# Second half of a vision tower: next slot's rows normalised one slot ahead, attention polynomials in front of the low halves, values behind the scores, three gelu high halves cast by VectorE

## The chip, the core and the metric

The kernel runs on one core of a Trainium2 chip. The metric is the device time of one execution in microseconds. Before the change it is 833.44 us, the median of 3 runs (833.27 to 834.65). Engines are named as in the profile: PE (TensorE, matrix products; PEld its weight loads), DVE (VectorE), ACT (ScalarE), POOL (GpSimd), SP (the queue of transfers).

## The reference

64 images of 128 x 128 become 64 tokens each of 256 features. Four residual steps follow: softmax attention with a learned choice of keys, a routed feed-forward with 8 experts, causal "polymax" attention, and a gelu feed-forward with ternary weights.

```python
h = tok(x)                                  # patches of 16x16 times W, + b
h = h + sparse_softmax_attn(layernorm(h))   # 16 heads, 25 of 64 keys kept
h = h + routed_ffn(layernorm(h))            # 2 of 8 experts, plus shared silu ffn
# polymax attention
q, k, v = split(layernorm(h) @ W_attn)
att = q @ k.T / 4, causal
att = (x > 0 ? x**2 + 1 : x in [-100, 0] ? -0.01 * x + 1 : 0) / 1000
h = h + (att @ v) @ W_proj
# gelu feed-forward, w_t = sign(w) * (|w| > 0.5 * mean|w|)
z = layernorm(h)
g = gelu((z / (rms(z) + 1e-8)) @ w_up_t.T)
h = h + (g / (rms(g) + 1e-8)) @ w_down_t.T
```

## The kernel before

The 4096 tokens lie in SBUF as `H`, 32 tiles of 128 rows. Four tiles (8 images) are a slot; there are 8 slots. Phase A takes each slot through embedding, softmax attention and the shared part of the routed step. Phase B, from about 437 us, takes each slot `g` through the polymax attention (B1 projections, B2 scores, polynomials, values, output projection) and the gelu feed-forward (B3). The whole `H` is complete before phase B, apart from 8 rows of slot 7 that slot 5 adds to. The experts' gates are worked off in slots 1 to 5.

There is no scheduler. Each engine has its program written out in order, in a function `slot_B` of its own, and semaphores join the five programs. `slot_B(0)` and `slot_B(1)` are written out, slots 2 to 4 are a loop, and slots 5, 6, 7 are written out again. `routed` is "first" in slot 1, "batch" in 2 to 4, "last" in 5. The stages overlap: in slot `g` PE still multiplies slot `g - 1`'s gelus by the down weights, and it makes slot `g + 1`'s projections and first scores.

PE's order in slot `g`: `B2_scores` of tiles 2, 3 (L690, L443); the down product of slot `g - 1`, tiles 0, 1, by the high halves of the gelus (`down_part`, L751); `gram` (L740), whose diagonal gives the mean squares of the gelus; the down product by the low halves (L751); `B2_values` of tiles 0, 1 (L707); transposes of the normalised rows of slot `g + 1` (L368); `B2_proj` (L717); the down product of tiles 2, 3 (L763); the gates' turn (L624); keys and queries of slot `g + 1` (L378); the experts' sums (L613); values 2, 3; first value projection (L327); `B2_proj` (L717); gates (L633); other value projections; transposes for B3 (L368); scores 0, 1 of slot `g + 1`; the up product (L730), one of 8 parts per gelu.

Every number is split in two 16-bit halves for PE. Of the gelus, `g32[f]` (f = 0 to 7) holds the result of ACT's gelu (L1055), `G_hi` the high half, cast by ACT (`g_high`, L1046), `G_lo` the low half, a subtraction on DVE (`g_parts`, L1728). The down product by high halves waits for `gh_out` at each `f`, `gram` for `gl_out`.

The rows of slot `g + 1` are normalised at the start of slot `g`: `stats3` on DVE (L1252, L1257, L1260), the power -1/2 on POOL (`p_rstd`, L1130), minus mean times that on DVE (`minus_mean3`, L1641), then four ACT instructions that write `xn1` (`a_norm3`, L993). PE's transposes wait for them. ACT then copies the turned values (`a_turned`, L998) and the transposes' high halves (`a_B1_x`, L1006); DVE subtracts for the low halves (`v_x3T`, L1652).

A tile's scores pass through ACT (`relus` L1032, `quads` L1042, `lins` L1037) and DVE (`poly`, L1665 and L1671). For tiles 0, 1 DVE does the squares (`v_quads`, L1677) and one linear part (`v_lin`, L1683). `norm4` on DVE (L1264) normalises the rows for B3, `a_B3_x` (L1093) and `v_x4T` (L1721) are the halves of their transposes; PE starts these transposes once ACT has emptied bank 7 of slot `g + 1`'s first values (`a_B1_v`, L1022).

## Time and profile before

| | us |
|---|---|
| median of 3 runs | 833.44 |
| the profiled execution | 830.7 |
| its span, first to last instruction | 828.7 |
| PE busy in the span | 703.1 (85%) |
| DVE busy | 617.9 (75%) |
| ACT busy | 428.4 (52%) |
| mean granted clock of TensorE | 0.926 of 2.4 GHz |

A slot of phase B is about 48 us. Times in the rows count from the start of the span. A timeline row gives the start, the length (of all that are merged in it), engine, line and operands, how many, and in brackets how long the engine stood idle ahead of it and who ended that. Instructions overlap a little in issue, so a duration is best read as the distance to the next start. A granted clock of 1.00 is 2.4 GHz, of 0.50 it is 1.2 GHz. PE shows fp32 products of one tile as two rows' worth each (x8 for four).

### The profile page before, as it was taken

The numbers are of one execution on the slowest core, as the hardware profiler recorded it, in microseconds if no ns is written. First come the engines' busy times: TensorE is split into PE (matmuls) and PEld (weight loads), VectorE is DVE, ScalarE is ACT, GpSimd is POOL, SyncE is SP. The second block draws the span as 40 slices with busy tenths as digits, with TensorE's granted clock in tenths as the row PEclk, the third lists the DMA queues.
The fourth block names the chain that finished last, engine by engine and source line by source line (L and its number), as shares of the span: only waits on it lengthen the run. The fifth ranks groups of instructions, "written<-read, shape, count | busy, mean of one in ns | idle before, by whom it ended". The sixth has DMA issues, their size and how long they took to land.

```text
span 828.7 us, 26974 instructions
## 1 busy us (share of the span) xinstructions
PE 703.1 (85%) x11581; PEld 495.5 (60%) x11581; DVE 617.9 (75%) x1393; ACT 428.4 (52%) x653; POOL 85.5 (10%) x76
## 2 busy tenths in 40 slices
PE   5878999999999999947756889899898989888766
PEld 4565766667676767634454556575566656465534
DVE  6676979787888888786595578968877786677543
ACT  4535454555555554544214575938566493656413
POOL 0100212121212020100000000000000000000000
PEclk9889999999999999977865999999998999999959
DMA  9034202020202002000000000000000000000000
GB/s 320 20 127 131 78 0 76 0 76 0 76 0 76 0 0 103 3 1 1 1 1 2 2 3 28 3 27 2 25 0 0 25 2 27 2 28 2 27 3 27
DMA packets 8546, 27.40 MB, mean 33 GB/s; under 512 B 3616, under 2 KB 4384, under 8 KB 6944
## 3 DMA queue, kind: packets, MB, share of 16 engines
q1 hardware_dynamic: 8480, 26.42, 8.8%
q8 instruction: 53, 0.87, 0.4%
q14 instruction: 13, 0.11, 0.0%
HBM read 22.22 MB, written 4.19 MB: 32 GB/s over the span
## 4 chain that ended last, share of the span: by engine, by line
PE 42%; issue 22%; DVE 21%; ACT 9%; POOL 2%; SPq 2%; DMA 1%; DVEq 0%; POOLq 0%; ACTq 0%
PE PS L378 7%; PE PS L327 6%; PE PS L389 5%; PE PS L488 4%; PE PS L717 3%; PE PS L368 3%; PE PS L477 3%; PE PS L432 3%; DVE mx L1343 3%; DVE Pm L1349 3%; PE PS L763 2%; PE PS L443 2%; SPq L307 2%; DMA work<-in_x 1%; PE PS L345 1%
## 5 line engine op out<-in xcount | busy, mean ns | idle before, releaser
L368 PE MATMUL PS<-ident_s,xn 128*128 128x128 f32 x256 | 50.3, 311 | 33.5 <-DVE xn L1264 16.5
L919 ACT ACTIVATE PT<-PS 128x512 f32<-128x512 f32 x64 | 36.7, 596 | 70.1 <-PE PS L477 70.1
L730 PE MATMUL PS<-xT,wqkv_h 128*128 128x512 f16 x256 | 63.1, 391 | 5.7 <-ACT w_s L1055 4.2
L368 PEld LDWEIGHTS PS<-ident_s,xn 128*128 128x128 f32 x256 | 32.0, 150 | 46.8 <-DVE xn L1264 15.5
L327 PE MATMUL PS<-tokW_h,w_s 128*128 128x256 f16 x504 | 58.5, 273 | 0.0
L912 ACT ACTIVATE Pm<-Pm 128x1024 f32<-128x1024 f32 x32 | 33.1, 1054 | 46.8 <-DVE Pm L1349 46.8
L327 PEld LDWEIGHTS PS<-tokW_h,w_s 128*128 128x128 f16 x504 | 48.7, 98 | 5.8
L443 PE MATMUL PS<-kM,qT 32*64 32x128 f32 x2048 | 50.2, 285 | 0.0
L378 PE MATMUL PS<-xT,wat_h 128*128 128x512 f16 x192 | 46.2, 400 | 4.5 <-DVE xT L1652 4.5
L730 PEld LDWEIGHTS PS<-xT,wqkv_h 128*128 128x128 f16 x256 | 22.6, 100 | 44.1 <-ACT w_s L1055 17.7
L1252 DVE BATCH_NORM_STATS2 st<-H 128x6 f32 (+1 forms) x128 | 46.3, 414 | 2.5
L477 PE MATMUL PS<-ident_s,Pm 128*128 128x128 f32 x256 | 41.1, 297 | 7.3 <-DVE Pm L1349 7.0
L1689 DVE TENSOR_TENSOR H<-H,PS 128x512 f32<-128x512 f32 (+1 forms) x16 | 11.0, 687 | 48.0 <-PE PS L717 48.0
L1130 POOL TENSOR_TENSOR rstd<-ve,mhalf 128x4 f32<-128x4 f32 x16 | 16.1, 1008 | 275.7 <-DVE ve L1260 275.7
L488 PE MATMUL PS<-vbuf,PT 128*64 128x34 f32 x1024 | 41.6, 233 | 3.4 <-ACT PT L919 3.4
L488 PEld LDWEIGHTS PS<-vbuf,PT 128*64 128x64 f32 x1024 | 36.1, 145 | 13.3 <-ACT PT L919 7.5
L1343 DVE TENSOR_REDUCE mx<-PS 128x16 f32<-128x1024 f32 x32 | 39.0, 1218 | 5.3 <-PE PS L443 5.3
L443 PEld LDWEIGHTS PS<-kM,qT 32*64 32x64 f32 x2048 | 42.8, 136 | 0.0
L717 PE MATMUL PS<-wpr_s,xT 128*128 128x256 f32 x128 | 41.4, 481 | 1.4 <-ACT xT L998 1.4
L1349 DVE TENSOR_TENSOR Pm<-PS,mx 128x1024 f32<-128x1024 f32 x32 | 39.2, 1225 | 3.5
L1728 DVE TENSOR_TENSOR work<-w_s,work 128x512 f16<-128x512 f32 x48 | 32.2, 688 | 11.2 <-ACT work L1046 11.2
L378 PEld LDWEIGHTS PS<-xT,wat_h 128*128 128x128 f16 x192 | 19.1, 102 | 28.8 <-issue 9.5
(250 smaller groups left out, 1610.9 us busy)
## 6 DMA issues: line engine op xcount, KB each, us to landing
work<-in_x SPq DMA_DIRECT2D x7, 1536.0 KB, 6.3
out<-H SPq DMA_DIRECT2D x8, 512.0 KB, 2.6
w_s<-in_w SPq DMA_DIRECT2D x3, 1024.0 KB, 6.9
work<-in_x SPq DMA_DIRECT2D x3, 512.0 KB, 5.7
wup_s<-in_wup SPq DMA_DIRECT2D x1, 1024.0 KB, 6.4
wdn_s<-in_wdn SPq DMA_DIRECT2D x1, 1024.0 KB, 8.4
w_s<-in_tokW SPq DMA_DIRECT2D x3, 256.0 KB, 4.1
wup_s<-in_wqkv SPq DMA_DIRECT2D x1, 768.0 KB, 7.7
```

The source lines that it names most:

```text
L327: m = pe.matmul(dst, halves_[xi][:, k, rows], w[:, wi, k, cols], start=(n == 0), stop=(n == 3 * chunks - 1))
L368: m = pe.transpose(PS[:, bank, t * P:(t + 1) * P], xn[:, t, c * P:(c + 1) * P], ident_s[:, :])
L378: m = pe.matmul(PS[0:cols, bank, :], w[:, wi, c, col:col + cols], x[xi][:, c, 0:TOK], start=(n == 0), stop=(n == 3 * C - 1))
L389: m = pe.matmul(PS[:, bank, :], w[:, wi, c, col:col + P], x[xi][:, c, 0:TOK], start=(c == 0 and wi + xi == 0), stop=(c == C - 1 and xi == 1))
L443: m = pe.matmul(PS[b * L:(b + 1) * L, i, hb + c * P:hb + (c + 1) * P], left[r, c, at:at + L], right[r, c, :, at:at + L], start=False, stop ...
L477: m = pe.transpose(PS[:, TURN_BANKS[t][half], hp * P:(hp + 1) * P], Pm[:, t % 2, at:at + P], ident_s[:, :])
L488: m = pe.matmul(PS[b * L:(b + 1) * L, 6 + t % 2, hp * 2 * VW:(hp + 1) * 2 * VW], PT[:, t % 2, hp, b * L:(b + 1) * L], Vb[:, 2 * t + b, hp, ...
L717: m = pe.matmul(PS[:, bank, (t % 2) * E:(t % 2 + 1) * E], yT[:, t, c, :], wpr_s[:, c, :], start=(c == 0), stop=(c == C - 1))
L730: m = pe.matmul(PS[:, UP_BANKS[f % 3], :], wup_h[:, c, f * P:(f + 1) * P], part[:, c, :], start=(k == 0), stop=(k == 2 * C - 1))
L1252: dve.bn_stats(st_[:, t, :], H[:, TILES * g + t, :]).then_inc(in_st, 1)
L1343: dve.tensor_reduce(mx[:, t % 2, :].rearrange("p (i h) -> p i h", i=4), PS[:, 0:4, hb:hb + 256].rearrange("p i (h k) -> p i h k", k=L), AX ...
L1349: dve.tensor_tensor(Pm[:, t % 2, :].rearrange("p (i h k) -> p i h k", i=4, k=L), PS[:, 0:4, hb:hb + 256].rearrange("p i (h k) -> p i h k", ...
```

## The change

1. `stats3`, `p_rstd`, `minus_mean3` and `a_norm3` for slot `g + 2` are done in slot `g` (slots 0 to 5) and not for slot `g + 1` at its start. On DVE the statistics stand behind `norm4(g, 0)`, the last step behind `stats4(g, 1)`; on ACT the four instructions stand between `a_turned(g, 1)` and `a_B1_v(g + 1, 0)`. In slot 5 all of it comes after the rows that the routed step adds, and ACT's part behind `a_B1_v(6, 0)`.
2. In DVE's order `poly(g + 1, 0)` and `poly(g + 1, 1)` stand in front of all of `g_parts`.
3. In PE's order `B2_values(g, 0)` stands in front of the down product by high halves.
4. `G_hi` of f = 5, 6, 7 is cast by DVE inside `g_parts`, each with a wait of its own, and no longer by ACT.
5. `v_x3T` and `silus` stand together in front of `weighted_hots` and `projected`.

```diff
+        ACT_HIGH = 5
...
                 for f in range(NF):
                     if high and t == 0:
-                        pe.wait_ge(gh_out, NF * g + f + 1)
+                        if f < ACT_HIGH:
+                            pe.wait_ge(gh_out, ACT_HIGH * g + f + 1)
+                        else:
+                            pe.wait_ge(ghv_out, (NF - ACT_HIGH) * g + f - ACT_HIGH + 1)
...
                 if prev:
                     pe.wait_ge(g_ok, NF * g)
+                    B2_values(g, 0)
                     for t in (0, 1):
                         down_part(g - 1, t, G_hi, True)
...
                     pe.wait_ge(racc_ok, 1)
-                B2_values(g, 0)
+                    B2_values(g, 0)
...
             def g_high(g, f):
-                act.wait_ge(g_ok, NF * g + f + 1)
-                act.activation(G_hi[:, f, :], g32[f], ACT.Copy).then_inc(gh_out, 1)
+                if f < ACT_HIGH:
+                    act.wait_ge(g_ok, NF * g + f + 1)
+                    act.activation(G_hi[:, f, :], g32[f], ACT.Copy).then_inc(gh_out, 1)
...
-                if nxt:
+                if not prev:
                     a_norm3(g + 1)
                 a_turned(g, 0)
...
                 a_turned(g, 1)
+                if ahead and routed != "last":
+                    a_norm3(g + 2)
                 if nxt:
                     a_B1_v(g + 1, 0)
                 if routed in ("first", "batch"):
                     routed_tanh(g, 0)
+                if routed == "last":
+                    a_norm3(g + 2)
                 a_B3_x(g)
...
                 for f in range(f0, f1):
-                    dve.wait_ge(gh_out, NF * g + f + 1)
+                    if f < ACT_HIGH:
+                        dve.wait_ge(gh_out, ACT_HIGH * g + f + 1)
+                    else:
+                        dve.wait_ge(g_ok, NF * g + f + 1)
+                        dve.tensor_copy(G_hi[:, f, :], g32[f]).then_inc(ghv_out, 1)
+                        dve.wait_ge(ghv_out, (NF - ACT_HIGH) * g + f - ACT_HIGH + 1)
                     dve.tensor_tensor(G_lo[:, f, :], g32[f], G_hi[:, f, :], ALU.subtract)\
...
-                if nxt:
-                    stats3(g + 1)
                 if prev:
                     mean_squares(g - 1)
-                if nxt:
+                else:
+                    stats3(g + 1)
                     minus_mean3(g + 1)
                 if routed in ("batch", "last"):
                     silus(g - 1)
+                if nxt:
+                    v_x3T(g + 1)
+                if routed in ("batch", "last"):
                     weighted_hots(g)
                 projected(g, 0, 5)
...
                 norm4(g, 0)
+                if ahead and routed != "last":
+                    stats3(g + 2)
                 projected(g, 1, 4)
                 stats4(g, 1)
+                if ahead and routed != "last":
+                    minus_mean3(g + 2)
...
+                if routed == "last":
+                    stats3(g + 2)
+                    minus_mean3(g + 2)
                 v_x4T(g)
                 if nxt:
                     v_quads(g + 1, 0)
                     v_quads(g + 1, 1)
                     v_lin(g + 1)
-                g_parts(g, 0, 4)
                 if nxt:
                     poly(g + 1, 0)
-                g_parts(g, 4, NF)
-                if nxt:
                     poly(g + 1, 1)
+                g_parts(g, 0, NF)
```

The left-out parts pass `ahead=False` to slots 6 and 7 on each engine and move POOL's `p_rstd` to stand between its two `p_ln4` (behind both in slot 5).

How the order reads, taken from slot 1, first before and then after in each pair. DVE at the end of slot 1, from the linear part of slot 2's first tiles; `th` and `hs` are the two tiles' polynomials, `work` the halves of the gelus:

```order
L1683 TENSOR_SCALAR late<-PS 128x1024
L1728 TENSOR_TENSOR work<-w_s,work 128x512 x4
L1665 SCALAR_TENSOR_TENSOR th<-u,th 128x1024
L1671 SCALAR_TENSOR_TENSOR Pm<-u,th 128x1024
L1728 TENSOR_TENSOR work<-w_s,work 128x512 x2
L1728 TENSOR_TENSOR work<-wqkv_h,work 128x512
L1728 TENSOR_TENSOR work<-tokW_h,work 128x512
L1665 SCALAR_TENSOR_TENSOR hs<-late,hs 128x1024
L1671 SCALAR_TENSOR_TENSOR Pm<-late,hs 128x1024
L1252 BN_STATS st<-H 128x6 x4
```

```order
L1696 TENSOR_SCALAR late<-PS 128x1024
L1678 SCALAR_TENSOR_TENSOR th<-u,th 128x1024
L1684 SCALAR_TENSOR_TENSOR Pm<-u,th 128x1024
L1678 SCALAR_TENSOR_TENSOR hs<-late,hs 128x1024
L1684 SCALAR_TENSOR_TENSOR Pm<-late,hs 128x1024
L1746 TENSOR_TENSOR work<-w_s,work 128x512 x5
L1744 CAST work<-w_s 128x512
L1746 TENSOR_TENSOR work<-w_s,work 128x512
L1744 CAST work<-wqkv_h 128x512
L1746 TENSOR_TENSOR work<-wqkv_h,work 128x512
L1744 CAST work<-tokW_h 128x512
L1746 TENSOR_TENSOR work<-tokW_h,work 128x512
```

Both polynomials now come first, then five subtractions, then cast and subtraction in turn three times; the four BN_STATS of the next slot's rows are no longer behind them.

ACT in slot 1, from the keys' and queries' copies to the gates' tanh (`wdn_s`); `vbuf` is the first value copy, `xn` the rows to be normalised:

```order
L1017 ACTIVATE kM<-PS,par_s 128x512 x4
L998 ACTIVATE xT<-PS 128x2x4x64
L1022 ACTIVATE vbuf<-PS 128x16x2x16
L988 ACTIVATE wdn_s<-wup_s 128x1024
L1093 ACTIVATE xT<-PS 128x512 x2
```

```order
L1022 ACTIVATE kM<-PS,par_s 128x512 x4
L1003 ACTIVATE xT<-PS 128x2x4x64
L998 ACTIVATE xn<-H,nm,rstd 128x256 x4
L1027 ACTIVATE vbuf<-PS 128x16x2x16
L993 ACTIVATE wdn_s<-wup_s 128x1024
L1103 ACTIVATE xT<-PS 128x512 x2
```

The four `xn` instructions now stand in front of `vbuf`, for which PE's next transposes wait.

PE at the start of slot 1, from the last scores:

```order
L443 MATMUL PS<-kM,qT 64x128 x16
L751 MATMUL PS<-tokW_h,work 128x256 x16
L740 MATMUL PS<-work 32x64 x128
L751 MATMUL PS<-tokW_h,work 128x256 x16
L707 MATMUL PS<-Pm,vbuf 32x64 x64
L368 MATMUL PS<-ident_s,xn 128x128 x8
```

```order
L444 MATMUL PS<-kM,qT 64x128 x16
L708 MATMUL PS<-Pm,vbuf 32x64 x64
L755 MATMUL PS<-tokW_h,work 128x256 x16
L741 MATMUL PS<-work 32x64 x128
L755 MATMUL PS<-tokW_h,work 128x256 x16
L369 MATMUL PS<-ident_s,xn 128x128 x8
```

The values (`Pm,vbuf`) moved from behind the down products to the front of them.

## Rows read from the trace of the kernel before

**Rows 1.** The page, section 1: busy time of each engine over the span.

```profile
PE 703.1 (85%) x11581; PEld 495.5 (60%) x11581; DVE 617.9 (75%) x1393; ACT 428.4 (52%) x653; POOL 85.5 (10%) x76
```

**Rows 2.** Timeline of PE, junction of slots 3 and 4, then slot 6 (start, length, idle before).

```profile
624.33 2.10 PE L751 MATMUL PS<-tokW_h,work 128*128 128x256 f16 x16 [0.37 <-ACT tokW_h L1055]
626.36 1.30 PE L740 MATMUL PS<-work 128*32 128x64 f16 x128
...
629.44 1.61 PE L707 MATMUL PS<-Pm,vbuf 64*32 64x64 f32 x128
633.58 0.33 PE L368 MATMUL PS<-ident_s,xn 128*128 128x128 f32 x1 [2.54 <-ACT xn L993]
...
734.96 0.76 PE L368 MATMUL PS<-ident_s,xn 128*128 128x128 f32 x5 [0.16 <-ACT xn L993]
735.56 1.89 PE L717 MATMUL PS<-wpr_s,xT 128*128 128x256 f32 x8
```

**Rows 3.** Timeline of DVE, same junction.

```profile
619.07 1.33 DVE L1728 TENSOR_TENSOR work<-w_s,work 128x512 f16<-128x512 f32 x2
...
622.33 1.22 DVE L1665 SCALAR_TENSOR_TENSOR th<-u,th 128x1024 f32<-128x1024 f32 x1
...
624.81 1.28 DVE L1728 TENSOR_TENSOR work<-w_s,work 128x512 f16<-128x512 f32 x2
...
629.61 1.40 DVE L1252 BATCH_NORM_STATS2 st<-H 128x6 f32 x4
```

**Rows 4.** Timeline of ACT, same junction.

```profile
624.00 0.70 ACT L1046 ACTIVATE work<-wqkv_h 128x512 f16<-128x512 f32 x1
...
631.75 1.01 ACT L1037 ACTIVATE late<-PS 128x1024 f32<-128x1024 f32 x1
632.93 2.08 ACT L993 ACTIVATE xn<-H,nm,rstd 128x256 f32 x4 [0.17 <-DVE nm L1641]
```

**Rows 5.** Groups of DVE instructions by form: busy, mean ns.

```profile
L1245 DVE TENSOR_SCALAR work<-wup_s,nthr 128x2048 f32<-128x2048 f32 x1 | 1.3, 1290 | 0.0
...
L1449 DVE CAST selb<-PS 128x512 bf16<-128x512 f32 x1 | 0.7, 681 | 0.0
...
L1234 DVE CAST cmaskb<-cmask_s 128x384 bf16<-128x384 f32 x1 | 0.4, 355 | 0.0
```

**Rows 6.** Timelines of PE, DVE and ACT before slot 3's gelus; DVE in slot 1.

```profile
611.01 1.09 PE L368 MATMUL PS<-ident_s,xn 128*128 128x128 f32 x6 [0.46 <-DVE xn L1264]
...
606.52 0.69 DVE L1689 TENSOR_TENSOR H<-H,PS 128x512 f32 x1 [2.13 <-PE PS L717]
...
608.46 0.16 DVE L1700 COPY vr<-mv 128x2 f32<-128x2 f32 x1
...
609.06 0.60 ACT L1022 ACTIVATE vbuf<-PS 128x512 f32<-128x512 f32 x1 [4.73 <-PE PS L327]
...
614.33 1.02 ACT L1032 ACTIVATE th<-PS 128x1024 f32<-128x1024 f32 x1
...
509.30 0.69 DVE L1689 TENSOR_TENSOR H<-H,PS 128x512 f32<-128x512 f32 x1 [0.38 <-PE PS L717]
```

**Rows 7.** Timelines of DVE and ACT before slot 5's gelus.

```profile
709.64 0.41 DVE L1634 TENSOR_TENSOR H<-H,PS 8x256 f32<-8x256 f32 x1 [1.19 <-PE PS L645]
...
710.40 0.60 ACT L1022 ACTIVATE vbuf<-PS 128x512 f32<-128x512 f32 x1 [8.78 <-PE PS L327]
...
714.34 1.02 ACT L1032 ACTIVATE th<-PS 128x1024 f32<-128x1024 f32 x1 [0.62 <-PE PS L443]
```

**Rows 8.** Windows: us, busy PE, PEld, DVE, ACT, POOL, granted clock, DMA, GB/s.

```profile
538.30:541.70 3.40, 3.40 (x11) 2.59 (x9) 0.89 (x1) 0.91 (x2) 0.00 (x0) 0.51 0.00 0
...
630.50:633.90 3.40, 0.86 (x55) 0.52 (x32) 2.86 (x18) 3.19 (x5) 1.98 (x2) 1.00 0.00 0
...
633.90:640.70 6.80, 6.60 (x22) 4.80 (x22) 3.17 (x5) 2.78 (x6) 0.00 (x0) 0.50 0.00 0
...
777.30:780.70 3.40, 3.40 (x11) 2.42 (x10) 0.22 (x1) 0.00 (x0) 0.00 (x0) 0.50 0.00 0
```

More of the change, by code:

```diff
@@ L778, in B3_down_last, with slot_B @@
                             m.then_inc(dn_mm, 1)
-            def slot_B(g, prev, nxt, routed=None):
+            def slot_B(g, prev, nxt, routed=None, ahead=True):
                 B2_scores(g, 2)
@@ L865, in _ @@
             slot_B(LAST - 2, True, True, routed="last")
-            slot_B(LAST - 1, True, True)
-            slot_B(LAST, True, False)
+            slot_B(LAST - 1, True, True, ahead=False)
+            slot_B(LAST, True, False, ahead=False)
             B3_down_last(LAST)
@@ L1061, in a_B3, with slot_B @@
                 g_high(g, NF - 1)
-            def slot_B(g, prev, nxt, routed=None):
+            def slot_B(g, prev, nxt, routed=None, ahead=True):
                 for t in (2, 3):
@@ L1121, in _ @@
             slot_B(LAST - 2, True, True, routed="last")
-            slot_B(LAST - 1, True, True)
-            slot_B(LAST, True, False)
+            slot_B(LAST - 1, True, True, ahead=False)
+            slot_B(LAST, True, False, ahead=False)
         @block.gpsimd
@@ L1177, in p_rg, with slot_B @@
                 pool.tensor_tensor(rg[:, :], msq[:, :], phalf[:, :], ALU.pow).then_inc(rg_ok, 1)
-            def slot_B(g, prev, nxt, routed=None):
-                if nxt:
-                    p_rstd(ve3_ok, g + 2, ve, rstd, rstd3_ok)
+            def slot_B(g, prev, nxt, routed=None, ahead=True):
                 if prev:
@@ L1191, in _ @@
             slot_B(LAST - 2, True, True, routed="last")
-            slot_B(LAST - 1, True, True)
-            slot_B(LAST, True, False)
+            slot_B(LAST - 1, True, True, ahead=False)
+            slot_B(LAST, True, False, ahead=False)
             p_rg(LAST)
@@ L1772, in slot_B @@
                     one_over_rms(g - 1)
-                if nxt:
-                    v_x3T(g + 1)
-                if prev:
                     ffn_out(g - 1)
@@ L1782, in slot_B @@
                 norm4(g, 0)
+                if ahead and routed != "last":
+                    stats3(g + 2)
                 projected(g, 1, 4)
                 stats4(g, 1)
+                if ahead and routed != "last":
+                    minus_mean3(g + 2)
                 if routed == "last":
@@ L1793, in slot_B @@
                     routed_rows_in()
+                if routed == "last":
+                    stats3(g + 2)
+                    minus_mean3(g + 2)
                 v_x4T(g)
@@ L1845, in _ @@
             slot_B(LAST - 2, True, True, routed="last")
-            slot_B(LAST - 1, True, True)
-            slot_B(LAST, True, False)
+            slot_B(LAST - 1, True, True, ahead=False)
+            slot_B(LAST, True, False, ahead=False)
             mean_squares(LAST)
```

8 lines of the change are left out of this document (5 added, 3 removed).

## The prediction

> **What bounds the kernel now.** I read the page first, then the timelines of PE, DVE and ACT over one slot of phase B, and last the windows with the granted clock. PE is busy for 703.1 of 828.7 us [rows 1], and within a slot it rests at few places, so a change pays only where it moves PE. I measure everything from the start of ACT's first relu of the next slot (614.33 [rows 6]), call that t, and follow slot 3 into slot 4. Behind the last scores, which end 0.37 before 624.33, so at 623.96, PE does 16 down products with high halves in 2.03, gram and low halves in 3.08 (626.36 to 629.44) and the values in 1.61, without a break, and ends at 631.05 [rows 2]. Then it stands for 2.54 until the rows of the next slot are normalised. That wait is a chain: DVE's statistics start at 629.61, behind the second polynomial [rows 3], POOL and one DVE step follow, and ACT starts its four normalisations at 632.93, 2.08 us for four [rows 4]. PE's transposes go at ACT's pace for the first few. In slot 6 the last five take 0.60 (734.96 to 735.56) [rows 2], that is 0.12 each; all eight at ACT's pace take about 2.0. So the output projection could start at 633.58 + 2.0 = 635.6, t + 21.2.
>
> The second thing to see is the clock. In the stretch in which PE idled (630.50 to 633.90) it was busy for 0.86, and right behind it the clock was at 0.50, 1.2 GHz, for 6.8 us [rows 8]. The projection there took 3.62 where it takes 1.89 in slot 6 [rows 2, 8]. I count five low stretches of 3.4 us in slots 2 to 5 and one in slot 7 at the same place (the first, the double one and the last are shown). A low stretch full of work costs 1.7, so the six cost about 10 us.
>
> **The change part by part: the junction of two slots.** The wait for the rows goes: they are ready a slot early. What is late next is the high halves. DVE starts its part behind the linear step at 619.07 [rows 3]. A polynomial lasts 2.48 (622.33 to 624.81), a subtraction 0.60 (half of 1.20 from 624.81 on, two with 0.09 of overlap). Two polynomials and five subtractions: 619.07 + 4.96 + 3.0 = 627.05. Only then comes the cast of f = 5.
>
> No row shows a cast of 128x512 between two SBUF tiles. From the sides: 128x512 out of PSUM took 0.68, 128x384 in SBUF 0.36, and 2048 elements of a one-input operation 1.29 [rows 5]. The line through the last two is 0.14 + 0.00056 per element, 0.42 for 512; I take that, since it rests on SBUF rows, and keep 0.36 and 0.69. (The Trainium skill, VectorE: DVE Perf Modes, section on the perf-mode tiers, has fp32 copies in SBUF at two elements per cycle and any PSUM operand of fp32 at one; by that the 0.68 row doesn't bear on this cast and the sum below stands; by the row alone it would be 5.7 higher. The trace agrees as far as the 1.29 goes.) A dependent pair starts 0.12 after the first ends (622.33 + 1.22 to 623.67). So the casts end at 627.05 + 0.42 = 627.5, then every 1.1 (0.42 + 0.12 + 0.60): 628.6 and 629.7.
>
> (The same page, in its section on the DRAIN, says that semaphores between chained operations cost nothing. The 0.12 in the row is against it. By the page f = 7 would land 0.2 to 0.3 earlier, some 2 us over seven junctions.)
>
> PE now does the values first, 623.96 to 625.56; both polynomials are done by 624.1, so they don't wait. Five high products until 626.2, then waits of 1.3, 1.0 and 1.0 for f = 5, 6, 7. With 9 products of 0.127 behind the last cast it is 630.9, with gram and low halves (the last low half is there at 630.5) 634.0, with eight unhindered transposes of 0.12 635.0. ACT isn't late: its last casts (624.00 to 625.2 [rows 4]) fall away, its last linear step ends 2 us before 632.8. So t + 20.7 instead of t + 21.2: 0.5 gained, not 4.5. For six junctions (slots 1 to 6) -3.3 with 0.55 each. Into slot 7 there is no row to be normalised; there PE waited only for ACT's linear step (632.8 in the same frame) and the turned values, 0.6 more, t + 19.1, against 634.0, t + 19.7, now: +0.6.
>
> **In front of the gelus.** ACT's four instructions now stand in front of `a_B1_v`, and wait for `minus_mean3`, which DVE issues behind the statistics of B3's second half. These end at 608.6 [rows 6], because `projected` waited 2.13 for PE. So ACT normalises from 608.8 to 610.9, and the value copy, before at 609.06, ends at 611.45. Behind the waiting instruction stand on ACT that copy, the tanh, the high halves of the transposes, then the relus and gelus. PE waits for the copy before it transposes: it resumed fully at 611.01 after 0.46, now it starts all eight at 611.5. ACT: tanh 1.0, high halves as the transposes end (613.6), value copy 0.5, tanh 1.0, relu at 615.1 instead of 614.33: +0.75. The gelus are ACT's pace, so nothing gives it back. The new statistics on DVE, 1.84 (like 629.61 to 631.45), fit into the 2.13 idle. Slots 0, 2, 3, 4: +3.0, slot 0 being an estimate by the others. In slot 1 `projected` had only 0.38 of idle in front of it [rows 6]; the first normalisation of B3 ends at 508.9 there. With `v_x3T` (1.2) taken out of the chain ahead it ends at 507.7, the statistics at 509.55, while the product is there at 508.7 (0.55 earlier than before): 0.85 of them is on the path, and slot 1 costs 0.75 + 0.85 = 1.6.
>
> In slot 5 the chain is serial: rows added at 709.64 to 710.05, statistics to 712.0, POOL 1.1, `nm` at 713.3, ACT 713.45 to 715.5, high halves 1.0, value copy 0.5, relu at 717.1 instead of 714.34 [rows 7]: +2.8.
>
> POOL's power for two slots ahead takes 1.0 between two of its own that stand 6 us apart: nothing. Nothing moves on SP. The end of slot 7 is PE's work; casts on an idle DVE hide beside it: nothing. `v_x3T` earlier frees DVE, but PE comes no earlier: nothing outside slot 1.
>
> **Sum without the clock:** -3.3 + 0.6 + 3.0 + 1.6 + 2.8 = +4.7. **The clock:** the idle time at a junction is now three waits of about 1 us with one product between, 3.3 in all, instead of 2.5 in one piece and thin transposes behind. PE is as empty as before for as long, so I expect the low stretches to stay in kind, and some to begin inside the idle time, where they cost less. I take one of the six as saved, -1.7, and as bounds none left (-10) and two more (+3.4), the second because slot 5 has a new wait of 3 us. In all +3.0: span 828.7 to 831.7, the profiled execution 830.7 to 833.7. The runs' median is 2.7 above that one execution, so I forecast 833.44 + 3.0, 836.4.
>
> **The rivals.**
> - The clock decides. If the three short waits don't bring the clock down, all low stretches go, 833.4 + 4.7 - 10 = 828. From fewer than three left on (4.7 / 1.7) the kernel is faster. For it: in slot 6 1.50 of idle and paced transposes left the clock up (the projection at 735.56 took 1.89). Against: PE's work between the waits is one product of 0.13 each.
> - The cast is slow, 0.69 as out of PSUM: 0.27 more for each of three casts at seven junctions, +5.7, 842. For it is only the one row with 512 elements; the SBUF rows speak against it.
> - The casts of f = 5 to 7 are on the path but the normalisation isn't: if ACT's early part were hidden (as it would be if `minus_mean3` came before 607), 3.0 + 1.6 fall away: about 832. Against it is the written order, which puts it behind `stats4`.
> - Gains and losses meet: three or four low stretches fewer, 833 to 834, no change.
>
> **How the numbers follow.** Forecast as described 0.47; slow cast 0.11; no change 0.20; clock up or norm hidden 0.22. A change under 0.2% (831.8 to 835.1) is one that a measurement can't tell from none. The forecast's own range is 834 to 840. The range for 8 in 10 takes in the next cases on both sides: 831 to 841.5. Faster 0.23, same 0.20, slower 0.57.
>
> **What would show it.** In the new profile: PE idle in front of the down products (L755), three times near 1 us per junction, released by DVE's casts; the casts at about 420 ns; no idle in front of the transposes of the next rows; ACT's `xn` instructions starting 0.1 behind `nm`, and PE idle 1.3 in front of B3's transposes in slots 0 to 4; some 3 us in slot 5 before the up product. The forecast is wrong if the casts end before PE wants them, if PE doesn't wait for the value copy, or if the clock stays at 1.00 across the junctions.

## The result, and the profile after

| | before | after |
|---|---|---|
| median of 18 runs, us | 832.89 (828.65 to 836.62) | 827.96 (824.38 to 834.26) |
| the profiled execution | 830.7 | 828.74 |
| its span | 828.7 | 826.6 |
| mean granted clock | 0.926 | 0.924 |

The ratio is 0.9946, with a 95% interval of 0.9924 to 0.9968: the change is 0.54% faster, 4.9 us between the medians. I had forecast 3 slower, and the range began at 831. The forecast was wrong in sign. The two profiled executions differ by 2.0 only, and their spans by 2.1, of which 1.8 arise before slot 1's first relu (470.90 and 469.09 us), nearly all in code that is the same; so single spans don't carry the comparison here, and I compare slots. Executions in the slower of the chip's two states are left out of the ratios here and below, so a ratio may differ a little from that of the medians.

The answer to [rows 1], busy time of each engine in the profile of after:

```profile
PE 697.0 (84%) x11581; PEld 493.8 (60%) x11581; DVE 626.1 (76%) x1417; ACT 413.7 (50%) x629; POOL 89.3 (11%) x76
```

24 casts of 0.4 have moved from ACT to DVE. PE does the same instructions in 6 us less, which no edit asks for. 3.0 of these lie ahead of slot 1's first relu, 1.9 behind slot 7's projection, where the clock was 0.80 and not 0.73, and only 1.1 in the slots between.

The junction of slots 3 and 4, PE's timeline of after, to be laid beside [rows 2]. Here t, the start of the first relu, is 610.49:

```profile
620.07 1.60 PE L708 MATMUL PS<-Pm,vbuf 64*32 64x64 f32 x128
621.60 0.72 PE L755 MATMUL PS<-tokW_h,work 128*128 128x256 f16 x5
623.59 0.28 PE L755 MATMUL PS<-tokW_h,work 128*128 128x256 f16 x1 [1.26 <-DVE work L1744]
624.65 0.28 PE L755 MATMUL PS<-tokW_h,work 128*128 128x256 f16 x1 [0.78 <-DVE work L1744]
625.71 2.10 PE L755 MATMUL PS<-tokW_h,work 128*128 128x256 f16 x9 [0.78 <-DVE work L1744]
627.74 1.68 PE L741 MATMUL PS<-work 128*32 128x64 f16 x128
629.36 1.92 PE L755 MATMUL PS<-tokW_h,work 128*128 128x256 f16 x16
631.12 1.04 PE L369 MATMUL PS<-ident_s,xn 128*128 128x128 f32 x8
631.99 1.89 PE L718 MATMUL PS<-wpr_s,xT 128*128 128x256 f32 x8
```

DVE's timeline there, which answers to [rows 3]:

```profile
620.10 3.09 DVE L1746 TENSOR_TENSOR work<-w_s,work 128x512 f16<-128x512 f32 x5
623.11 0.42 DVE L1744 CAST work<-w_s 128x512 f16<-128x512 f32 x1
623.56 0.69 DVE L1746 TENSOR_TENSOR work<-w_s,work 128x512 f16<-128x512 f32 x1
```

And the windows of after over PE's three waits and over what follows them, to be laid beside [rows 8]:

```profile
624.00:627.40 3.40, 1.97 (x10) 1.28 (x10) 2.31 (x5) 2.55 (x4) 0.00 (x0) 0.73 0.00 0
627.40:630.80 3.40, 3.40 (x144) 2.87 (x143) 1.19 (x9) 0.00 (x0) 0.44 (x1) 0.77 0.00 0
```

The wait for the rows is gone as forecast, and three waits for DVE's casts, at 0.42 each, stand in its place. (The Trainium skill, VectorE: DVE Perf Modes, section on the perf-mode tiers, gives an fp32 copy in SBUF the rate on which my 0.42 stood; the row agrees.) What is new is where the low clock falls. Here it begins 0.1 before the last wait ends (elsewhere between 0.1 after that and, in slot 7, 1.1 before it) and lies on nine products, 2.10 long, and on `gram`, 1.68; at full clock these take 1.16 and 1.34 (rows of the filled kernel below). In before it lay on the full projection, which at full clock takes 1.89:

```profile
636.18 3.62 PE L717 MATMUL PS<-wpr_s,xT 128*128 128x256 f32 x8
```

The step from the cast at 623.11 to its subtraction at 623.56 is 0.45, so a dependent pair behind a cast loses only 0.03 and not the 0.12 that I had read off a pair of polynomial steps.

In front of the gelus, ACT and PE in slot 3 of after, which answer to [rows 6]:

```profile
604.71 2.07 ACT L998 ACTIVATE xn<-H,nm,rstd 128x256 f32 x4 [4.50 <-DVE nm L1654]
606.69 0.58 ACT L1027 ACTIVATE vbuf<-PS 128x512 f32<-128x512 f32 x1
...
610.49 1.03 ACT L1037 ACTIVATE th<-PS 128x1024 f32<-128x1024 f32 x1
...
607.32 1.09 PE L369 MATMUL PS<-ident_s,xn 128*128 128x128 f32 x8 [1.10 <-ACT vbuf L1027]
```

I had PE idle for 1.3 here in slots 0 to 4. It is 1.1 in slots 2 to 4, but 1.7 in slot 1 and 4.7 in slot 0.

### The profile page after: what moved, and what is told of

Its sections match the earlier page's. It is cut to its first block, busy times and chain, and to the rows that moved or that the text cites. A ratio compares the mean times of both kernels' runs of the same rounds, so it can differ in the third digit from the quotient of the medians.

```text
span 826.6 us, 27023 instructions
## 1 busy us (share of the span) xinstructions
PE 697.0 (84%) x11581; PEld 493.8 (60%) x11581; DVE 626.1 (76%) x1417; ACT 413.7 (50%) x629; POOL 89.3 (11%) x76
## 4 chain that ended last, share of the span: by engine, by line
PE 47%; DVE 28%; issue 10%; ACT 9%; SPq 3%; DMA 1%; POOL 1%; DVEq 0%; ACTq 0%; POOLq 0%
PE PS L379 7%; PE PS L328 6%; PE PS L390 5%; DVE work L1746 4%; PE PS L489 4%; PE PS L755 3%; PE PS L718 3%; PE PS L369 3%; PE PS L767 3%; PE PS L478 3%; DVE mx L1356 3%; DVE Pm L1362 3%; PE PS L433 2%; DVE hs L1678 2%; DVE th L1678 2%
## 5 line engine op out<-in xcount | busy, mean ns | idle before, releaser
L731 PE MATMUL PS<-xT,wqkv_h 128*128 128x512 f16 x256 | 65.2, 403 | 8.9 <-DVE xT L1734 4.6
L369 PE MATMUL PS<-ident_s,xn 128*128 128x128 f32 x256 | 42.6, 298 | 25.2 <-DVE xn L1277 12.6
L755 PE MATMUL PS<-tokW_h,work 128*128 128x256 f16 x224 | 37.1, 315 | 18.1 <-DVE work L1744 18.1
L444 PE MATMUL PS<-kM,qT 32*64 32x128 f32 x2048 | 52.0, 293 | 0.0
L379 PE MATMUL PS<-xT,wat_h 128*128 128x512 f16 x192 | 44.5, 390 | 2.5 <-DVE xT L1665 2.5
L755 PEld LDWEIGHTS PS<-tokW_h,work 128*128 128x128 f16 x224 | 22.9, 110 | 28.2 <-DVE work L1744 22.7
L478 PEld LDWEIGHTS PS<-ident_s,Pm 128*128 128x128 f32 x256 | 29.7, 149 | 10.4 <-issue 8.4
L718 PE MATMUL PS<-wpr_s,xT 128*128 128x256 f32 x128 | 33.9, 412 | 0.7 <-ACT xT L1003 0.7
```

Of the source, the lines that this page charges most:

```text
L369: m = pe.transpose(PS[:, bank, t * P:(t + 1) * P], xn[:, t, c * P:(c + 1) * P], ident_s[:, :])
L379: m = pe.matmul(PS[0:cols, bank, :], w[:, wi, c, col:col + cols], x[xi][:, c, 0:TOK], start=(n == 0), stop=(n == 3 * C - 1))
L444: m = pe.matmul(PS[b * L:(b + 1) * L, i, hb + c * P:hb + (c + 1) * P], left[r, c, at:at + L], right[r, c, :, at:at + L], start=False, stop ...
L478: m = pe.transpose(PS[:, TURN_BANKS[t][half], hp * P:(hp + 1) * P], Pm[:, t % 2, at:at + P], ident_s[:, :])
L718: m = pe.matmul(PS[:, bank, (t % 2) * E:(t % 2 + 1) * E], yT[:, t, c, :], wpr_s[:, c, :], start=(c == 0), stop=(c == C - 1))
L731: m = pe.matmul(PS[:, UP_BANKS[f % 3], :], wup_h[:, c, f * P:(f + 1) * P], part[:, c, :], start=(k == 0), stop=(k == 2 * C - 1))
```

## The slots, kernel by kernel

Below, T1 is the time from a slot's first relu t to the next output projection (the junction, 21.2 in my text), T2 the time from that projection to the next t. "Clean" is a slot in which no window shows a low clock. Both are starts read off the timelines, and a T1 is counted to the slot in which it ends. The T1 column covers slots 2 to 6. The mean granted clock is that of the stretch from 484 to 755 us (slots 1 to 6); "no releaser" is PE's idle time there that the waits put down to nothing.

| kernel | ratio to before | T1 clean | T2 clean, slots 2 to 4 | mean clock | no releaser, us |
|---|---|---|---|---|---|
| before | 1 | 21.2 | none (25.8 in the runs without part 1) | 0.97 | 2.3 |
| after | 0.9946 | 20.4 (slot 2 alone); 20.2 in kernels made from it | 26.03 | 0.96 | 0.5 |
| part 1 alone | 0.9904 | 19.4 to 19.6 | 26.05 | 0.97 | 2.0 |
| part 2 alone | 0.9830 | 20.4 | 25.76 | 0.99 | 1.0 |
| parts 2, 3 alone | 0.9906 | 20.4 (slot 5), 21.0 and 21.3 (slots 2, 6) | 25.75 | 0.97 | 5.9 |
| part 4 alone | 1.0057 | none (22.6 to 23.2) | 25.76 | 0.96 | 0 |
| part 1 undone | 0.9983 | 21.7 to 21.9 | 25.76 | 0.97 | 1.0 |
| part 3 undone | 1.0164 | none (23.1 to 23.9) | 26.04 | 0.94 | 0 |
| part 4 undone | 0.9779 | 17.8 (slots 3 to 5) | 26.05 | 0.99 | 5.6 |

Before and after are nearly alike in the mean clock, but not in what a low stretch costs at a junction nor in how many there are. In slots 3 to 5 of after, the T1 of 20.2 becomes 21.4 to 21.6 with a low stretch and T2 isn't touched; in before, T1 of 21.2 becomes 21.85 and T2 rises from 25.8 to 26.7, 27.4 and 28.0. Per slot that is 1.3 against 1.5 to 2.9. On the other hand after has seven low stretches between 484 and 755 us and before five (two of them back to back), and one of double length stands in front of slot 7's projection (T1 22.09 instead of 19.15). The whole way from slot 1's first relu to slot 7's projection, and the rest behind it, first before and then after:

```profile
470.90:776.94 306.04, 272.76 (x5266) 184.38 (x5264) 232.27 (x491) 195.33 (x297) 25.02 (x25) 0.97 0.03 12
776.94:828.70 51.76, 34.36 (x408) 22.23 (x408) 22.91 (x60) 10.16 (x19) 3.02 (x3) 0.73 0.06 22
```

```profile
469.09:776.57 307.48, 271.64 (x5267) 185.40 (x5266) 237.73 (x502) 180.25 (x272) 27.86 (x24) 0.95 0.03 12
776.57:826.60 50.03, 32.42 (x410) 20.84 (x408) 23.91 (x63) 8.69 (x16) 3.02 (x3) 0.80 0.06 22
```

So in this pair the slots take 1.4 longer after the change, at a mean clock of 0.95 instead of 0.97, although the clean times make them about 1.2 shorter (the sum in the section on the prediction, without slot 0). In these two executions the low clock costs after some 2.6 more there, not less.

## The experiments

Each is compared with the kernel before, run on the same chip. The intervals are of the ratio to it. The medians of the kernel before lie between 830.59 and 832.89 from chip to chip, so two experiments are compared by their ratios.

**Part 1 alone** (next rows normalised a slot ahead, in the kernel before).

```diff
-                if nxt:
-                    stats3(g + 1)
                 if prev:
                     mean_squares(g - 1)
...
                 norm4(g, 0)
+                if ahead and routed != "last":
+                    stats3(g + 2)
```

> The kernel before with part 1 alone: rows normalised a slot ahead; the polynomials, the values and all eight casts (on ACT) stand as before. My theory T: the wait of 2.5 us for the rows is what held a junction, and the casts on DVE gave most of that back. Then a junction here loses the wait (2.54) and the paced transposes (about 0.7): 6 x -3.2 = -19, against it about +4.5 in front of the gelus (0.3 in four slots, 2.6 in slot 5): 15 to 18 us faster than before, near 817, also well faster than after. Rival R (the casts on DVE are what helps ACT, the rows alone bring little): within 3 us of the changed kernel or slower. Rival C (the time follows the low stretches of the clock): the wait gone, they go too, and it is 20 us or more faster than before.

Measured 823.1 against 831.05, ratio 0.9904 (0.9866 to 0.9941): 8 faster, half of what T said, and far from C. That is 3.5 faster than after by the ratios, whose intervals overlap, so R's number isn't excluded; its reason, that the casts on DVE help, falls with the runs on part 4 below. T overlooked what comes next. PE, then ACT, in the junction of slots 3 and 4:

```profile
629.04 1.27 PE L368 MATMUL PS<-ident_s,xn 128*128 128x128 f32 x8 [1.81 <-ACT late L1037]
...
625.89 1.02 ACT L1032 ACTIVATE hs<-PS 128x1024 f32<-128x1024 f32 x1 [1.59 <-DVE Pm L1678]
```

With the rows there, PE waits 1.81 for ACT's last linear step; ACT waited 1.59 for DVE's second polynomial, which stood behind all low halves. Parts 1 and 2 belong together.

**Parts 2 and 3 alone, and part 2 alone.** Both take the polynomials to the front in DVE's order; the first also takes the values to the front in PE's.

```diff
-                g_parts(g, 0, 4)
                 if nxt:
                     poly(g + 1, 0)
-                g_parts(g, 4, NF)
-                if nxt:
                     poly(g + 1, 1)
+                g_parts(g, 0, NF)
```

> The kernel before with parts 2 and 3 alone: both polynomials in front of the low halves, values in front of the down product; all casts on ACT, rows normalised at the start of the slot. Theory T: DVE's statistics for the next rows start at the same time as before, since the sum of its work ahead is the same, so PE's wait for the rows stays and takes the same end: no change, within 2 us of before. Rival R (the new order itself is the gain): 4 to 6 us faster. Rival C: only the place of the idle time matters to the clock, some us either way with the cleanly clocked junction unchanged.

> The kernel before with part 2 alone: both polynomials in front of all low halves, everything else as before. With part 3 beside it 7.6 us were gained, which I had not expected. Reading of that trace: in the kernel before DVE stood still twice for 0.31 behind a gelu's cast and the second polynomial came only behind all low halves; without that its statistics for the next rows start 0.84 earlier (t + 14.44 instead of 15.28), and so do the rows. Theory T: this is the whole gain: 5 to 7 us faster than before, the place of the values is worth nothing while PE waits for the rows. Rival V (the values in front are the gain): within 2 us of before.

Measured 823.45, ratio 0.9906 (0.9871 to 0.9941), for the two parts; 816.29, ratio 0.9830 (0.9802 to 0.9857), for part 2 alone. The first refutes T as it stood (no change): the low halves of f = 2, 3 had waited twice 0.31 for ACT's casts. The second is the surprise of the study, and twice what its T said: the same DVE work, a clean T1 of 20.4 in both, and 6 us less by the ratios. PE in the same junction, part 2 alone:

```profile
620.35 0.30 PE L740 MATMUL PS<-work 128*32 128x64 f16 x16 [0.30 <-DVE work L1728]
620.95 0.30 PE L740 MATMUL PS<-work 128*32 128x64 f16 x16 [0.30 <-DVE work L1728]
621.55 0.30 PE L740 MATMUL PS<-work 128*32 128x64 f16 x16 [0.30 <-DVE work L1728]
...
623.64 1.61 PE L707 MATMUL PS<-Pm,vbuf 64*32 64x64 f32 x128
625.38 0.33 PE L368 MATMUL PS<-ident_s,xn 128*128 128x128 f32 x1
```

Its windows, and behind them PE's wait and the windows of the kernel with parts 2 and 3:

```profile
620.60:624.00 3.40, 2.80 (x92) 2.21 (x86) 3.29 (x19) 3.07 (x4) 0.62 (x1) 1.00 0.00 0
624.00:627.40 3.40, 2.77 (x118) 2.01 (x104) 2.82 (x4) 2.68 (x6) 1.36 (x2) 1.00 0.00 0
```

```profile
630.34 0.33 PE L368 MATMUL PS<-ident_s,xn 128*128 128x128 f32 x1 [1.68 <-ACT xn L994]
```

```profile
627.40:630.80 3.40, 1.59 (x13) 1.02 (x10) 2.86 (x18) 2.39 (x5) 1.98 (x2) 1.00 0.00 0
630.80:634.20 3.40, 3.04 (x10) 2.41 (x11) 2.29 (x2) 2.64 (x5) 0.00 (x0) 0.62 0.00 0
```

With gaps of 0.30 (three) and 0.17 (three) a junction the clock stays at 2.4 GHz through slots 1 to 4 of part 2 alone; with the values in front, the wait for the rows stands in one piece of 1.68, and in slots 3 and 4 the clock falls to 1.2 GHz right behind it (T1 21.0, T2 26.8). These two slots are 3.1 of the 5.1 by which the two traces differ between slot 1's first relu and slot 7's projection. The rest isn't all the clock: with the values in front PE is idle for 5.9 without a releaser and not for 1.0, and slot 2, with a clean clock, has a T1 of 21.0. Of the 14.6 that part 2 alone brings, 6 x 0.85 = 5 is T1; the other 9 are close to the 10 at which the prediction had put the low stretches of before. All of these are gone from the junctions; one in slot 5, at 693 us, stands elsewhere. That it is the long gap which brought the clock down is not shown: see the runs with one cast and with part 1 undone.

**Part 4 alone, and part 4 undone** (the three casts).

```diff
-        ACT_HIGH = 5
+        ACT_HIGH = NF
```

> The kernel before with part 4 alone: f = 5, 6, 7 cast by DVE, its order and PE's as before. Theory T: three casts of 0.42 stand in DVE's chain ahead of the statistics for the next rows, which PE waits for: 1.3 later in six junctions: 6 to 9 us slower than before. Behind parts 1 and 2 the same casts cost 15, because PE asks for the halves at once there. Rival R (ACT's relief pays by itself): faster than before. Rival P (a cast costs the same wherever it stands): 15 slower.

> The changed kernel with all eight high halves cast by ACT again (part 4 undone). Theory T: PE's three waits in front of f = 5, 6, 7 (1.26, 0.78, 0.78) go, and nothing takes their place before the transposes: junction shorter by 2.5 to 2.8 in slots 1 to 7, about 17 us faster than after, 810 to 813. Rival R (ACT needs the relief): ACT's casts then end too late for f = 5 to 7, and it is the same as after or slower. Rival C: the waits gone, the low stretches of the clock go as well, and it is 25 us faster than after.

Part 4 alone: 835.55, ratio 1.0057 (1.0037 to 1.0077), 4.7 slower, T1 1.35 longer as T says, with a low stretch in every junction from slot 2 on; the total is below its 6 to 9, and P (15) is refuted. The changed kernel without part 4: 812.87, ratio 0.9779 (0.9741 to 0.9816), inside T's 810 to 813. Its junction has no wait left:

```profile
621.55 1.38 PE L741 MATMUL PS<-work 128*32 128x64 f16 x128
622.86 1.92 PE L755 MATMUL PS<-tokW_h,work 128*128 128x256 f16 x16
624.92 1.10 PE L369 MATMUL PS<-ident_s,xn 128*128 128x128 f32 x8
```

So by the ratios the casts on DVE cost 14 here and 5 where the rows are late anyway. That ACT had to be relieved is refuted.

**One cast on DVE instead of three.** In the changed kernel:

```diff
-        ACT_HIGH = 5
+        ACT_HIGH = 7
```

> The changed kernel with one high half cast by DVE (f = 7) and seven by ACT. All eight on ACT gave 812.9 where three on DVE gave 828.0. Theory T (what costs is that a cast on DVE stands behind two polynomials and all subtractions in order, so that the last one is late): 624.03 + 7 x 0.6 + 0.42 = 628.65 in the frame of slot 3, where three casts end at 629.7 and PE asks at about 627; so one cast alone costs over half of what three do: 7 x 1.1 faster than after, 819 to 822. Rival (each cast costs its own 0.42 and gap, in proportion): a third of the cost, near 818 or less. Rival (ACT is relieved by one cast, DVE has the room): as fast as all on ACT, 813.

Measured 816.76, ratio 0.9810 (0.9784 to 0.9835). T1 is 19.3 in slots 3 and 4, where T's chain with 5.3 behind the cast makes 19.6, and the total 2 below T's range: four fifths of the 14 come back. The wait is in one piece, and the clock stays up around it (1.00 in all windows from 617.8 to 628.0, 0.99 in the mean), although it is no shorter than the 1.68 above:

```profile
621.78 1.16 PE L755 MATMUL PS<-tokW_h,work 128*128 128x256 f16 x9 [1.73 <-DVE work L1744]
```

T gave the order of the effect (more than in proportion, one cast costs 1.5 of T1 and three cost 2.4), not the total.

**Part 1 undone** (parts 2 to 4 stay).

```diff
-                if not prev:
+                if nxt:
                     a_norm3(g + 1)
```

> The changed kernel with the next rows normalised at the slot's start again (parts 2 to 4 stay). Theory T: with the casts in DVE's chain the rows are ready 1.3 later than with parts 2 and 3 alone, at t + 21.8 instead of 20.2 to 20.4 here: 6 x 1.4 = 8.4, less what part 1 costs in front of the gelus (3.6 in all): about 5 slower than after, near 833, the same as before the change. Rival A (part 1 costs what I forecast, 7.4 in all): 1 slower than after, 829. Rival C (low stretches as in the kernel before, on the projection): 8 to 10 slower.

Measured 829.14, ratio 0.9983 (0.9963 to 1.0003): 3 slower than after by the ratios, whose intervals just meet, where T said 5 and A 1; C is refuted. The junction is T's (21.84, forecast 21.8), and T2 is 25.76: part 1 costs 0.28 in slots 2 to 4, so rival A is wrong in its reason though nearest in its number. What makes T's 5 into 3 is likely the clock: slots 2 to 4 have no low stretch here, and in after slots 3, 4 and 5 have one each. Yet the waits for the casts are the same as in after, with paced transposes behind them. PE's waits and two windows in the junction of slots 3 and 4:

```profile
626.54 0.28 PE L755 MATMUL PS<-tokW_h,work 128*128 128x256 f16 x1 [1.27 <-DVE work L1737]
...
628.67 1.16 PE L755 MATMUL PS<-tokW_h,work 128*128 128x256 f16 x9 [0.78 <-DVE work L1737]
```

```profile
624.00:627.40 3.40, 1.56 (x69) 0.96 (x48) 3.37 (x7) 3.34 (x5) 0.00 (x0) 1.00 0.00 0
627.40:630.80 3.40, 2.42 (x122) 1.94 (x122) 3.33 (x12) 1.65 (x2) 0.00 (x0) 1.00 0.00 0
```

So the length and number of the waits don't settle by themselves whether the clock falls.

**Part 3 undone** (the values behind the low halves again, in the changed kernel).

```diff
                     pe.wait_ge(g_ok, NF * g)
-                    B2_values(g, 0)
...
                         down_part(g - 1, t, G_lo, False)
+                    B2_values(g, 0)
```

> The changed kernel with the values back behind the down product's low halves (part 3 undone). Theory T, from starts in the trace of after: the last cast is ready at t + 15.2 whatever PE does before; 9 products 1.1, gram 1.3, low halves 1.8, values 1.55, transposes 0.9 behind it make t + 21.8 instead of 20.2: 1.5 in seven junctions, about 10 us slower than after, near 838. Rival C (PE's waits move to another place and the clock stays up, as it did where part 2 stood alone): the 10 are given back by it, and it is the same as after or faster.

Measured 845.79, ratio 1.0164 (1.0137 to 1.0191), 18 slower than after by the ratios and 8 beyond T; C is refuted. PE and the windows:

```profile
633.23 0.28 PE L755 MATMUL PS<-tokW_h,work 128*128 128x256 f16 x1 [2.81 <-DVE work L1744]
...
635.36 2.10 PE L755 MATMUL PS<-tokW_h,work 128*128 128x256 f16 x9 [0.78 <-DVE work L1744]
```

```profile
630.00:633.40 3.40, 0.59 (x5) 0.25 (x3) 3.37 (x7) 3.37 (x4) 0.00 (x0) 1.00 0.00 0
633.40:636.80 3.40, 1.84 (x9) 1.13 (x9) 2.56 (x5) 2.32 (x3) 0.00 (x0) 0.69 0.00 0
```

The waits are 4.4 a slot and every junction up to slot 6 has its low stretch, two of them 6.8 long. Part 3 is worth 18 behind parts 1, 2 and 4, and costs 6 behind part 2 alone. It pays where it fills a wait.

**Part 5 undone** (`v_x3T` behind `one_over_rms` again).

> The changed kernel with the low halves of the next rows (v_x3T) back behind one_over_rms, as before the change (part 5 undone). My prediction put this part at nothing outside slot 1. From the trace of after: in slot 0 PE's keys and queries start 2.07 earlier, but the time is lost again at B3's transposes, whose rows come last; so at most 1 us there, and in slots 1 to 5 the wait of PE for the halves may come back at 0.3 to 0.5 each. Theory T: 1 to 3 us slower than after. Rival (the part is worth nothing): same within 0.5.

Measured 827.65, ratio 0.9943 (0.9922 to 0.9964), the same as after: the rival holds and T (1 to 3 slower) doesn't. In slot 0 the low halves bring PE forward, as I had not seen, but it waits for B3's rows in any case; in slot 1 T2 is 0.5 longer. The prediction's "nothing outside slot 1" holds for the total.

**Filling PE's waits.** To test the clock by itself, PE multiplies something that nobody reads, in front of its waits in the changed kernel.

```diff
+                            fill(9 if f == ACT_HIGH else 6)
                             pe.wait_ge(ghv_out, (NF - ACT_HIGH) * g + f - ACT_HIGH + 1)
```

> The changed kernel with 21 more products a slot (9, 6, 6), whose result nobody reads, put by PE into a free part of bank 6 in front of its waits for f = 5, 6, 7. At 0.127 each they fill the waits of 1.26, 0.78, 0.78 and should move nothing by themselves. Theory C (PE's idle time at the junction brings the low stretch behind it, which costs 1.1 in slots 3 to 5 and more in slot 7): the low stretches at the junctions go, 4 to 8 us faster than after. Rival (the low stretches come anyway, wherever PE is thin): same as after, or up to 2 slower by products that end late.

> The changed kernel with 10 products of 512 columns (4, 3, 3) in front of the waits for f = 5, 6, 7, in place of the 21 products of 256: about the same length of filled time, half the instructions. The 21 kept the clock up through slots 1 to 5, but PE stood for 10.8 us without a releaser in the profile, and in the loop's last turn its instructions were loaded again, which in no other run happened. Theory I (the instructions cost it, by their number: the loop no longer stays in PE's store): with 20 fewer no loads in the loop's second and third turn, the stalls back at 0.5 to 3, and the time 3 to 6 us faster than after, from the low stretches that go. Rival (filling costs by itself, or the loop is too long already): at or above after's time.

With 21 products of 256 columns: 837.88, ratio 1.0044 (1.0009 to 1.0079), 8 slower than after by the ratios where C said 4 to 8 faster, and yet the low stretches between 484 and 700 are all gone in the profiled execution. With 10 of 512: 825.6, ratio 0.9928 (0.9901 to 0.9955). That is 1.5 under after by the ratios, too little to tell, and short of Theory I's 3 to 6. But the junction of slots 3 and 4 in the second is the cleanest comparison of the study, since its waits and after's end at the same time (the product behind the last cast starts at 625.70 here and at 625.71 in after):

```profile
624.75 0.81 PE L749 MATMUL PS<-wqkv_h 128*128 128x512 f16 x3
625.70 1.16 PE L761 MATMUL PS<-tokW_h,work 128*128 128x256 f16 x9
626.78 1.34 PE L741 MATMUL PS<-work 128*32 128x64 f16 x128
628.06 1.92 PE L761 MATMUL PS<-tokW_h,work 128*128 128x256 f16 x16
...
630.69 1.68 PE L718 MATMUL PS<-wpr_s,xT 128*128 128x256 f32 x7
```

The projection starts at 630.69 and not at 631.99: 1.30 is what the clock takes from after at this junction. In the profile it was given back in slot 2 and late: 4.7 without a releaser, and low stretches in slots 5 and 6. What the 21 products cost is told below.

**The normalisation moved out of the way**, in three forms: ACT's four instructions behind the first turned values of the next slot, with slot 7's statistics late (first in the changed kernel, then with all casts on ACT); `minus_mean3` earlier on DVE; and slot 7's alone late.

```diff
                 a_turned(g, 0)
+                if prev and nxt:
+                    a_norm3(g + 1)
```

> The changed kernel with ACT's four normalisations moved behind the first turned values of the next slot, where ACT stands idle for 5.17, and slot 7's statistics in slot 5 put behind the high halves' subtractions, its last step behind the linear part on DVE. Theory T: the wait of 1.1 in front of B3's transposes (4.7 in slot 0) and that of 3.1 in slot 5 go; they cost 0.3 in slots 2 to 4 and 2.6 in slot 5: 4 to 5 us faster than after, and slot 0 some 0.3 to 2 more. Rival S (the relu's time is set by other work of ACT, so that the moved step is worth nothing outside slot 5): 2.6 faster. Rival N (the normalisation moved there meets the junction's own copies): no faster than after.

> Two edits of the changed kernel together: all casts on ACT, and the four normalisations behind the first turned values with slot 7's statistics late. Theory T: the gains add, since the second is worth what the relu of the next slot gains (0.2 in slots 2 to 4, 2.4 in slot 5, by its own run): 3 us faster than with the casts on ACT alone, near 810. Rival N (with ACT's casts back, the normalisation at the junction stands in front of the copies that PE waits for): the gain of 3 is lost or turned, 813 or more.

Measured 826.14, ratio 0.9935 (0.9906 to 0.9965), for the first, and 817.5, ratio 0.9827 (0.9803 to 0.9852), for the second. In the changed kernel T2 falls as forecast (25.83, and 27.3 in slot 5 where after has 29.6), but the total moves by 1, which can't be told from none, and not by 4 to 5; four of the five junctions from slot 1 to 5 keep a low stretch. T holds for the waits and not for the time. With all casts on ACT rival N holds: PE then waits for ACT at each row (1.04, 3 x 0.16), T1 is 19.8 and not 17.8, and the edit costs 4 by the ratios. It seems that ACT's idle 5.17 at the junction was only there because PE was late.

```diff
                 projected(g, 1, 4)
-                stats4(g, 1)
                 if ahead and routed != "last":
                     minus_mean3(g + 2)
+                stats4(g, 1)
```

> The changed kernel with all casts on ACT and with the last step of the statistics for slot g + 2 directly behind projected(g, 1), in front of B3's second statistics. ACT then normalises 1.2 earlier, its value copy ends before PE asks for it, and B3's own second rows come 0.2 later. Theory T: 0.2 to 0.3 of the four slots' cost in front of the gelus goes, 0 to 1 us faster than with all casts on ACT (812.9): cannot be told from it. Rival (the power of POOL isn't there yet, DVE then stands still in front of this step and B3's rows come late): 2 to 4 us slower.

> The fastest kernel so far (all casts on ACT, last step of the statistics early: 810.1) with slot 7's normalisation taken out of slot 5's chain: its statistics beside PE's up product, ACT's four instructions behind the linear steps of slot 6. Theory T: in slot 5 the wait of 3.08 in front of the up product goes (2.4, with the low stretch that follows it up to 4), and slot 6's junction pays 0.3 to 1.3 back: 1.5 to 3 us faster, 807 to 808.6. Rival N (as with all rows normalised there, PE waits at ACT's pace and the gain is gone): 810 to 812.

Measured 810.13, ratio 0.9746 (0.9721 to 0.9772), and 809.3, ratio 0.9724 (0.9697 to 0.9750). T2 in slots 2 to 4 is 25.76, all of part 1's cost gone; in the second kernel slot 5 loses its wait of 3.08 (T2 29.05 from 31.41) and pays part back in slot 6's junction (T1 21.4 from 20.5). Neither edit's own gain can be told from none: the intervals of 0.9779, 0.9746 and 0.9724 overlap in turn, and 809.3 lies between T (807 to 808.6) and N (810 to 812). The last kernel is 2.8% under before and 2.2% under after.

## Why the prediction was wrong

The sum without the clock was +4.7; the same sum with the measured terms is about -1.4. So without any clock the terms already change the sign. The measured -4.9 leaves a remainder of -3.5, and the clock's term was -1.7.

- **Junction of slots 1 to 6, -0.55 each: right in kind, mis-sized.** T1 was to be 20.7 and is 20.2 to 20.4, from 21.2: -1.0 in slots 2 to 5, -1.1 in slot 1 (by the filled kernels; 22.56 before, 21.43), -0.2 in slot 6 (by the run with part 5 undone, 21.04, whose low stretch there lies among the gelus). -5.3 instead of -3.3. I added durations where starts count: the last cast came 0.15 earlier than reckoned, and what follows it takes 5.0 (1.1 + 1.3 + 1.75 + 0.9) instead of 5.3.
- **Junction into slot 7, +0.6: not there.** 19.14 before, 19.15 in the filled kernel without a low stretch (21 products).
- **Normalisation ahead of the value copy, 0.75 in four slots: the step that failed most.** The wait is where I put it (transposes at +7.06 from the projection, forecast 7.1), but from the value copy to the relu ACT takes 3.80 from start to start and I had 4.2, by adding durations that overlap. It costs 0.28 in slots 2 to 4, and slot 0 is 0.2 faster: +0.6 instead of +3.0.
- **Slot 1, +1.6:** T2 23.65 to 24.64, +1.0. **Slot 5, +2.8:** 29.6 where the kernel with part 4 alone, at a clean clock, has 27.3, +2.3; it held best.
- **The casts** at 0.42 with waits of 1.3, 1.0, 1.0: the row has 0.42, and 1.26, 0.78, 0.78. The slow cast is refuted.
- **The clock, -1.7: a term taken as a guess from bounds of -10 to +3.4.** The low stretches stayed, as I said, and some begin inside the idle time, as I said; I counted one of six as saved and did not price the others. In slots 3 and 4 one costs 1.3 in after and 1.5 to 2.9 in before, but after has more of them, and over all slots of the profiled pair the low clock costs after some 2.6 more. The mean granted clock doesn't favour after either: 0.923 over its 18 runs, 0.924 over the 63 runs of the kernel before that stand beside the experiments. So no run shows the clock to have given the -3.5; it is a remainder. The profiled execution of before lies 2.2 under its median and that of after 0.8 over its own, and only these two have windows. A run's clock does bear on its time: among after's 18 the one with 0.931 took 824.4, that with 0.912 took 834.3.

The rival "the clock decides" was nearest in number (828), by luck: its reason was that the low stretches would go, and they did not.

So the mechanism was right and the sign wrong: small costs taken too high mostly by one habit, durations in place of starts, a gain taken too low by the same, and a clock term that was not worked out. Shown by runs are T1 and T2 with each part taken away, 1.30 for the clock at one junction, and the 14 of the casts. Open is where the remaining -3.5 between the medians comes from, and why the clock falls at one junction and not at another with the same waits.

## What to carry to other kernels

Build chains from start to start of the trace, never from durations: 0.1 to 0.5 a chain came to 4.4 (junctions and value copies) of the 6.1 by which the sum without the clock was off. When a wait is removed, ask in the same trace which engine feeds the next one; part 1 and parts 2 and 3 bring 8 and 7.6 apart and 18 together, and a relief of an engine that wasn't late (the casts) ate 14 of them. And don't read the clock off the waits: price it by what work would lie under it, here 1.3 on nine products and `gram` against 1.7 on the projection, and give its number a range, since one wait of 1.68 had a low stretch behind it and one of 1.73 had not.

## What the runs showed of the hardware

**The same waits came with and without the half clock.** In the profiled execution of after PE waits 1.15, 0.78 and 0.78 in slot 2 and the clock stays at 1.00; in slot 3 it waits 1.27, 0.78 and 0.78 and the clock is at 0.50 for 3.4 us, from 577.8. With part 1 undone the waits of slot 3's kind leave it at 1.00 in three slots.

**PE's instructions seem to arrive in pieces of 16 KB over a queue of their own, with PE at times ahead of them.** "Idle without a releaser" is 0.5 in after and 5.6 with no wait left: there it appears at the low halves and at `gram`, 128 short products in a row. PE in slot 2 with all casts on ACT, the loop's first turn, and then that queue from 515 to 545 us (packets, MB, share of 16 engines):

```profile
531.22 1.27 PE L755 MATMUL PS<-tokW_h,work 128*128 128x256 f16 x10 [1.24 <-issue]
532.42 1.13 PE L741 MATMUL PS<-work 128*32 128x64 f16 x117
535.30 0.27 PE L741 MATMUL PS<-work 128*32 128x64 f16 x11 [1.76 <-issue]
```

```profile
q8 instruction: 4, 0.07, 1.1%
```

In the loop's second and third turn (580 to 655 us) that kernel, before, after and the kernel with 10 wide products have no such packet and no such idle time. With 21 products more in the loop there are eight, and PE's idle times come back in the third turn:

```profile
q8 instruction: 8, 0.13, 0.7%
```

```profile
622.45 0.37 PE L691 MATMUL PS<-cmaskb,keyb 32*64 32x256 bf16 x16 [2.68 <-issue]
...
629.15 0.33 PE L708 MATMUL PS<-Pm,vbuf 64*32 64x64 f32 x12 [1.97 <-issue]
```

A likely reading is that the loop's code stays with the engine until 21 products more make it too long. That the packets are PE's code is inferred from where they come; no run changed the code's length alone. Nor does this explain the 8 us that filling cost: of that kernel's twelve runs three took 828.6 to 829.5 and nine 834.1 to 843.8, and the profiled execution with these packets is one of the three. What the nine have more has no trace.

**Waits at a junction seem to hide those idle times.** With after's waits of 2.8 a junction 0.5 of them is left, without them 5.6. So taking the casts from DVE brought 2.4 of T1 or more in slots 3 to 5, and none in slot 2 (20.4 and 20.6).
